# Diagonal score tiles split by query halves, softmax division and row statistics moved to VectorE, loads of the Wo stage reordered

## The reference

```
q, k, v = x@Wq.T+bq, x@Wk.T+bk, x@Wv.T+bv          # 16 heads
scores  = (q . k) * 64**-0.5 * exp(-alpha*|i-j|)
attn    = softmax(scores) ; out = (attn @ v) @ Wo.T + bo
x = layernorm(x + out)
xq, wq  = fp4_quant_dequant of blocks of 16 along the last dim (scale = max|x|/6)
h = silu(xq @ wgate_q.T) * (xq @ wup_q.T)           # width 2816
x = layernorm(x + quant(h) @ wdown_q.T)
```

## Time and profile before

| | us |
|---|---|
| median of 3 runs (lowest to highest) | 1411.84 (1408.74 to 1412.66) |
| the profiled execution, time | 1410.03 |
| its span on the slowest core (cores 1391.1 to 1408.5) | 1408.5 |
| PE busy | 1183.9 (84%) |
| DVE busy | 1060.4 (75%) |
| ACT busy | 707.0 (50%) |
| POOL busy | 300.7 (21%) |

### The profile page before, as it was taken

One profiled execution on the slowest core, in us unless ns is written; L12 is line 12 of the kernel. 1 busy time (PEld: TensorE's weight loads), 2 busy tenths in 40 slices (PEclk: granted clock), 3 DMA queues, 4 the chain that ended last, 5 costly groups with the idle time before them and its releaser, 6 DMA issues.

```text
span 1408.5 us, 18014 instructions; the slowest of 8 cores (1391.1 to 1408.5 us)
## 1 busy us (share of the span) xinstructions
PE 1183.9 (84%) x5283; PEld 441.4 (31%) x5344; DVE 1060.4 (75%) x1360; ACT 707.0 (50%) x803; POOL 300.7 (21%) x513
## 2 busy tenths in 40 slices
PE   3959888888888888887886493899999999999993
PEld 1312222222222222222221131344444444444441
DVE  2778888888989887887897421549988888888870
ACT  1038767677777776777797343652211221122212
POOL 2002223232222232222322132420000110011001
PEclk9979999999999998999999696999999999999997
DMA  9564334344444533543446919683333242333321
GB/s 150 114 140 128 112 93 119 97 107 101 122 118 105 121 104 96 129 108 92 126 108 159 245 55 308 210 272 91 111 84 84 73 121 84 79 84 92 92 61 55
DMA packets 179315, 167.27 MB, mean 119 GB/s; under 512 B 141842, under 2 KB 141842, under 8 KB 178324
## 3 DMA queue, kind: packets, MB, share of 16 engines
q1 hardware_dynamic: 164132, 127.97, 34.1%
q0 software_dynamic: 15088, 38.16, 11.5%
HBM read 111.30 MB, written 34.34 MB: 103 GB/s over the span
## 4 chain that ended last, share of the span: by engine, by line
PE 45%; DVE 18%; issue 15%; DMA 11%; ACT 5%; POOL 3%; SPq 1%; DVEq 1%; POOLq 0%; ACTq 0%
PE ps L953 12%; PE ps L545 8%; PE ps L412 7%; PE ps L1022 6%; PE ps L466 4%; PE ps L485 4%; ACT PT L530 3%; DVE SD L498 3%; PE ps L407 3%; DMA den_scr<-AV 2%; DVE fr L232 2%; DMA cD<-den_scr 2%; DVE hb L237 2%; POOL stat L813 2%; DMA hb<-x 1%
## 5 line engine op out<-in xcount | busy, mean ns | idle before, releaser
L530 ACT ACTIVATE PT<-ps,tab 128x1024 bf16<-128x1024 f32 x384 | 410.0, 1117 | 115.4 <-PE ps L466 114.2
L545 PE MATMUL ps<-PT,V 128*128 128x512 bf16 x992 | 296.4, 392 | 6.9 <-issue 2.7
L466 PE MATMUL ps<-Q,KT 64*128 64x512 bf16 x768 | 180.6, 391 | 31.4 <-ACT PT L530 26.7
L485 PE MATMUL ps<-Q,KT 64*128 64x512 bf16 x256 | 100.1, 391 | 106.4 <-DVE SD L498 97.1
L498 DVE TENSOR_TENSOR SD<-ps,tab 128x512 f32<-128x512 f32 x256 | 174.0, 680 | 20.3 <-PE ps L485 13.9
L953 PE MATMUL ps<-wgT,x1qT 128*128 128x512 bf16 (+1 forms) x768 | 167.8, 362 | 3.5 <-ACT sg L963 3.0
L953 PE MATMUL ps<-wuT,x1qT 128*128 128x512 bf16 (+1 forms) x768 | 167.8, 362 | 0.0
L412 PE MATMUL ps<-xTs,wqk 128*128 128x512 bf16 x495 | 145.5, 408 | 24.9 <-DMA xTs<-xT 17.1
L1022 PE MATMUL ps<-wdT,hqT 128*128 128x512 bf16 x704 | 156.3, 382 | 2.7 <-DMA hqT<-hq 2.7
L530 ACT ACTIVATE PT<-SD 128x1024 bf16<-128x1024 f32 x128 | 135.6, 1059 | 7.7 <-DVE SD L498 7.5
L805 ACT ACTIVATE junk<-ring 128x1024 bf16<-128x1024 f32 x22 | 23.2, 1054 | 214.3 <-DVE ring L1030 205.1
(11 more groups left out here) (84 smaller groups left out, 1365.4 us busy)
## 6 DMA issues: line engine op xcount, KB each, us to landing
ring<-x_scr SPq DMA_DIRECT2D x32, 512.0 KB, 5.3
wst<-wg SPq DMA_DIRECT2D x22, 512.0 KB, 3.8
wst<-wu SPq DMA_DIRECT2D x22, 512.0 KB, 3.7
wst<-wd SPq DMA_DIRECT2D x16, 704.0 KB, 4.1
recD<-rec_scr POOLq DMA_DIRECT2D x64, 128.0 KB, 3.6
out<-ring POOLq DMA_DIRECT2D x16, 512.0 KB, 6.3
wg_scr<-wtr SPq DMA_DIRECT2D x22, 256.0 KB, 2.0
wu_scr<-wtr SPq DMA_DIRECT2D x22, 256.0 KB, 2.0
```

The lines of the kernel that those rows point to most:

```text
L466: tok = op(TE, k0, lambda e, r0=r0, half=half: e.matmul(out=pt[:, half * 512:(half + 1) * 512], lhsT=KT[hp % 2][r0:r0 + 64, kt * 128:(kt + ...
L485: tok = op(TE, k0, lambda e: e.matmul(out=pt, lhsT=KT[hp % 2][r0:r0 + 64, kt * 128:(kt + 1) * 128], rhs=QR[u % 3][0][r0:r0 + 64, :], start ...
L530: f = op(AC, k0, lambda e: e.activation(out=PT[ri], in_=src, func=AF.Exp, scale=scl), [tok, pt_free[ri], t_tab])
L545: tok = op(TE, ka, lambda e, half=half: e.matmul(out=ps_ab[half], lhsT=VV[g][:, kt, hp % 4, 8 * half:8 * half + 128], rhs=PT[ri][:, half * ...
```

## The change

1. **Diagonal tiles.** The 512 queries are halved. For each half only two of the four key tiles lie on the diagonal; the other two are before or after all its queries. These go the factored way, with a third prescaled copy of the queries (table strM, which adds one DVE instruction per unit and head pair): a step "F" holds two key tiles of 256 queries and takes two exponentials of 128x512. The rest, step "D", still passes through SD: 4 DVE multiplies of 128x512 per unit instead of 8, 2 exponentials instead of 4. Matmuls of these steps have 256 columns, twice as many of them.
2. **Division** (L636 now) on DVE, at key ka+9.5, where ka is the key of the unit's last product with V (the last unit's at ka+23).
3. **Quantisers** are no longer spread evenly: `fill_gaps` replays the recorded DVE instructions with nominal durations (`durs`) and puts the chain's instructions where the nominal time leaves room.
4. **Wo stage.** The statistics come from `bn_stats` and `bn_aggr` on DVE (`layer_norm_w`), two small DVE instructions, two on POOL. The x row buffers wrow lie where the weight quantisers' buffers were, and the rows are loaded as soon as those are free. The loads of wuT follow after tiles 9, 11, 13, 14 and 15. The first product of stage G into hb waits for all stores of x1. `start_x1` of tiles 0 and 1 comes after tiles 7 and 10 (before: 4 and 6).
5. SBUF places and small tables follow from it.

```diff
-            tiles[u] = [k for i in range(4) for k in nd[3 * i:3 * i + 3] + [di[i]]]
+            nd = [("N", k) for k in range(NTT) if k not in di]
+            steps[u] = (nd[0:3] + [("F", di[0], di[1])] + nd[3:6] + [("D", di[0], di[1])]
+                        + nd[6:9] + [("F", di[2], di[3])] + nd[9:12] + [("D", di[2], di[3])])
+        BUF = [(j - (j > 7)) % 2 for j in range(16)]
...
+        durs = []
...
-                for n, ok, st in ((1, c > 0, strB), (2, c < 3, strA)):
+                for n, ok, st in ((3, True, strM), (1, c > 0, strB), (2, c < 3, strA)):
...
-                    rhs=Qs[r0:r0 + 64, :], start=True, stop=True,
-                    tile_position=(r0, 0)), need if half == 0 else [], signal=half == 1)
-            slot_last[hp] = tok
-            q_last[u] = tok
-            s_tok[(u, j)] = (tok, pt, None, k0, buf)
+            if need_d:
+                dt = bank(DB)
+                q0 = 256 * (b // 2)
+                h = j % 4
+                tok = d_a[0] = score(u, 4 * qc + b, h, 0, q0, q0 + 256,
+                                     dt[:, 256 * h:256 * h + 256], k0, need_d, True)
+            if st[0] == "N":
+                order = (1, 0) if j % 4 == 0 else (0, 1)
+                for half in order:
+                    tk = score(u, st[1], half, n, 0, 512, pt[:, half * 512:half * 512 + 512],
+                               k0, need if half == order[0] else [], half == order[1])
+            else:
+                q0 = 256 if j == 3 else 0
+                for i, k in enumerate(st[1:]):
+                    for half in range(2):
+                        c0 = 512 * half + 256 * i
+                        tk = score(u, k, half, n, q0, q0 + 256, pt[:, c0:c0 + 256], k0,
+                                   need if i + half == 0 else [], i + half == 2)
+            s_tok[(u, j)] = (tk, k0)
...
-            tok = op(TE, k0, lambda e: e.matmul(
-                out=pt, lhsT=KT[hp % 2][r0:r0 + 64, kt * 128:(kt + 1) * 128],
-                rhs=QR[u % 3][0][r0:r0 + 64, :], start=True, stop=True,
-                tile_position=(r0, 0)), need)
...
-            f = op(DV, km, lambda e: e.tensor_tensor(
-                out=SD[n][:, half * 512:(half + 1) * 512], in0=pt, in1=toep[:, x0:x0 + 512],
-                op=ALU.mult), [tok, t_tab, old, t_bo if u == 0 else None])
...
+            if j % 4 == 1:
+                n = b // 2
+                old = sd_exp[n]
+                km = max(k0 + 0.3, old.at + 0.02 if old is not None else -1e9)
+                x0 = 128 * (1 - b % 2)
+                f = dv(km, 0.69, lambda e: e.tensor_tensor(
+                    out=SD[n][:, 512 * (b % 2):512 * (b % 2) + 512].rearrange(
+                        "p (h q) -> p h q", h=2),
+                    in0=dt.rearrange("p (h q) -> p h q", h=2),
+                    in1=toep[:, x0:x0 + 256].unsqueeze(1).broadcast_to([128, 2, 256]),
+                    op=ALU.mult), [tok, t_tab, old, t_bo if u == 0 else None])
...
-                sd_exp[n] = f
-            else:
-                free_tok[buf], free_at[buf] = [f], k0
+                src = sc_ps[BUF[j]]
+                if st[0] == "N":
+                    m = 4 * qc - st[1] - 1 if st[1] < 4 * qc else st[1] - 4 * qc - 4
+                    scl = (sclB if st[1] < 4 * qc else sclA)[:, m:m + 1]
+                    f = op(AC, k0, lambda e: e.activation(
+                        out=PT[ri], in_=src, func=AF.Exp, scale=scl), need)
...
+                    for i in range(2):
+                        m = 1 - i if j == 3 else i
+                        scl = (sclB if j == 3 else sclA)[:, m:m + 1]
+                        part = lambda t, i=i: t.rearrange("p (h q) -> p h q", h=2)[
+                            :, :, 256 * i:256 * i + 256]
+                        f = op(AC, k0, lambda e, scl=scl, part=part: e.activation(
+                            out=part(PT[ri]), in_=part(src), func=AF.Exp, scale=scl),
+                            need if i == 0 else [], signal=i == 1)
+                free_tok[BUF[j]], free_at[BUF[j]] = [f], k0
...
                      + [t.at + 0.02 for t in need if t is not None])
...
+            if st[0] == "N":
+                prods = [(h, st[1], 512 * h, 0, 512) for h in range(2)]
+            else:
+                q0 = 256 if j in (3, 15) else 0
+                prods = [(h, k, 512 * h + 256 * i if st[0] == "F" else 256 * h + 512 * i, q0, 256)
+                         for i, k in enumerate(st[1:]) for h in range(2)]
+            for i, (h, k, c0, q0, w) in enumerate(prods):
+                tok = op(TE, ka, lambda e, h=h, k=k, c0=c0, q0=q0, w=w: e.matmul(
+                    out=ps_ab[h][:, q0:q0 + w], lhsT=VV[g][:, k, hp % 4, 8 * h:8 * h + 128],
+                    rhs=PT[ri][:, c0:c0 + w], start=first, stop=j > 12,
+                    skip_group_check=True), need if i == 0 else [], signal=i == len(prods) - 1)
             av_at[0] = ka
...
                     [t4, norm.get(u - 1)], sem=d_n4, k=16)
+            km = ka + 9.5 if u < NU - 1 else ka + 14.0 + 9.0
             for half in range(2):
                 lo = slice(64 * half, 64 * half + 64)
-                norm[u] = op(PO, ka + 5.8 + 0.1 * half, lambda e, half=half, lo=lo: e.tensor_tensor(
+                norm[u] = dv(km + 0.1 * half, 0.68, lambda e, half=half, lo=lo: e.tensor_tensor(
                     out=attnT[lo, hp, qc * QC:(qc + 1) * QC], in0=AVs[s][half][lo, :],
                     in1=recD[lo, :], op=ALU.mult), [t5])
...
-        spans = [(-30.0, at(0, 16))] + [(at(u, 1.9), at(u, 16.4)) for u in range(1, NU)]
-        spans[-1] = (spans[-1][0], at(NU - 1, 6))
-        room = sum(y - x for x, y in spans)
-
-        def place(f):
-
-            f *= room
-            for x, y in spans:
-                if f <= y - x:
-                    return x + f
...
+        U_US, P_US = 1.27, 0.95
+        t_of = lambda a: a * U_US if a > 0 else a * P_US
+        k_of = lambda t: t / U_US if t > 0 else t / P_US
+        durs.sort()
+        def fill_gaps(slack):
+            t, i, out, ka = t_of(-18.0), 0, [], -18.0
+            while i < len(durs) and durs[i][0] <= ka:
+                i += 1
+            for _, _, F in chunks:
+                for d, _ in quant_chain(wst[0][:, 0:F], wst[0][:, 0:F], wqo[0][:, 0:F], F, qr, qs):
+                    while i < len(durs) and t + d > t_of(durs[i][0]) + slack:
+                        t = max(t, t_of(durs[i][0])) + durs[i][1]
+                        ka = durs[i][0]
+                        i += 1
...
+                    nk = durs[i][0] if i < len(durs) else 1e9
+                    ka = max(ka + 1e-5, min(k_of(t), nk - 0.005))
+                    out.append((ka, k_of(t)))
+                    t += d
+            return out, k_of(t)
+        for slack in (0.2, 0.4, 0.6, 0.8, 1.0, 1.5, 2.0, 3.0, 5.0, 8.0):
+            places, q_end = fill_gaps(slack)
+            if q_end < at(NU - 1, 2):
+                break
+        places = iter(places)
+        nxt = next(places)
         w_read, w_tr, w_st = {}, {}, {}
...
+        ln_w = [0]
+        ln_done = [None] * 4
+        def layer_norm_w(x, tk):
+            o = 16 * (ln_w[0] % 4)
+            ln_w[0] += 1
+            c = lambda i, j=1: stat2[:, o + i:o + i + j]
+            for h in range(2):
+                tk, t = urgent(dve[0], 0.6, lambda e, h=h: e.bn_stats(
+                    out=c(6 * h, 6), in_=x[:, 512 * h:512 * h + 512]), [tk, ln_done[o // 16]])
+            tk, t = urgent(t, 0.1, lambda e: e.bn_aggr(out=c(12, 2), in_=c(0, 12)), [tk])
+            tk, t = urgent(t, 0.1, lambda e: e.tensor_scalar(
+                out=c(0), in0=c(12), scalar1=-1.0, scalar2=None, op0=ALU.mult), [tk])
+            tk, t = urgent(t, 0.1, lambda e: e.tensor_scalar(
+                out=c(1), in0=c(13), scalar1=EPS, scalar2=None, op0=ALU.add), [tk])
+            tk = fop(PO, t + 0.05, lambda e: e.tensor_tensor(
+                out=c(14), in0=c(1), in1=nhalf, op=ALU.pow), [tk])
+            tk = fop(PO, t + 0.06, lambda e: e.tensor_tensor(
+                out=c(15), in0=c(0), in1=c(14), op=ALU.mult), [tk])
+            t += 1.0
+            n = fop(AC, t + 0.05, lambda e: e.activation(
+                out=x, in_=x, func=AF.Identity, scale=c(14), bias=c(15)), [tk])
+            ln_done[o // 16] = n
+            return n, t + 1.3
         y_free = [(None, 0.0), (None, 0.0)]
         y_n = [0]
...
                 a = max(X0 - 8.0, pe[0] - 12.0,
                         w_free[s].at + 0.01 if w_free[s] else 0.0)
-                ld = fop(SP, a, lambda e: e.dma_start(out=row, in_=x_r[tt]),
-                         [w_free[s]] if w_free[s] else gate, sem=d_wl2[s], k=16)
+                ld = op(SP, a, lambda e: e.dma_start(out=row, in_=x_r[tt]),
+                        [w_free[s]] if w_free[s] else [prev] + t_ws, sem=d_wl2[s], k=16)
             y = y_n[0] % 2
...
             y_free[y] = (rt, t)
-            nt, t = layer_norm(row, t + 0.05, rt)
+            nt, t = layer_norm_w(row, rt)
```

(21 more changed lines are left out.)

199 lines of the change are left out of this document (89 added, 110 removed).

## The result

| | before | after |
|---|---|---|
| median of the runs (lowest to highest) | 1412.25 us | 1481.47 us (1476.12 to 1558.27) |
| ratio, 95% interval | | 1.0481 (1.0451 to 1.0511), slower |
| profiled execution, span | 1410.0, 1408.5 | 1476.12, 1474.5 |
| first copy of ps_ab | 111.61 | 110.12 |
| 29 periods, each | 648.9, 22.4 | 722.1, 24.9 |

A forecast was written before the change was run, and what follows sets the result against it. It took the kernel as bound by waits, the largest PE's 97.1 us for DVE's diagonal multiplies. Terms 7 + 0 + 1 - 29 + 13 = -8 gave 1402, against the median 1404 us; range 1377 to 1447.

The forecast's parts named there:

- R: Attention unit: time from DVE's copy of ps_ab to the division, through the wait for recD; taken as 14.7 us.
- PE's side: Attention: PE's wait for SD should be small, with a new one for the copy or projection banks there.
- Rival D: Attention, faster: only load counts, the wait is hidden, period about 20.3 us; sum -76, 1336 us; chance 0.05.
- the last leg: Attention, from recD's issue to the division: DVE now idle there, so 14.7 taken between 15.4 and 13.35.
- rival C: Attention, faster: the chain is quick, 13.8 us from copy to division; sum -34, 1378 us; chance 0.15.
- W: Attention unit: DVE's work from the division to the next copy; forecast 7.9 us each (7.3 to 8.9).
- +7: Attention, 29 periods: 29 x 14.7 + 230 = 656 us against 648.9.
- Rival A: Attention, slower: the quantiser's own transfers, tied to the unit, meet recD; R = 15.5, sum +16, 1428 us; chance 0.30.
- The burst: Attention, period at the burst of loads: reciprocal at +27, division about +38, 43.7 us against 44.0: 0.
- The last period: End of attention: R + 1.2 + 4.5 against 19.45 us: +1.
- The Wo stage: Between attention and G: 69 us, just over PE's 64, against 98.2: -29.
- The start of G: G(0) to G(1): second x1qT lands late behind wdT, at G+34 against G+21.2 before: +13.

The follow-up runs named there:

- e1: The changed kernel with the two divisions of a unit given back to POOL: 1370.91 us, ratio 0.9716.
- e3: The changed kernel with the division still on DVE but 17.5 keys behind the copy instead of 9.5, behind the next unit's copy: 1356.49 us, ratio 0.9619.
- e5: The changed kernel with the division on DVE 7.5 keys behind the copy instead of 9.5: 1538.53 us, ratio 1.0888.
- e5b: The changed kernel with the division on DVE 11.5 keys behind the copy instead of 9.5: 1413.92 us, ratio 0.9985.
- e11: e7 with the reciprocal and division of the last three units further back and the quantiser spread evenly: 1330.08 us, ratio 0.9443.
- e4: The changed kernel with the quantiser spread evenly by key instead of put into gaps, division still at 9.5 keys: 1483.08 us, ratio 1.0506.
- e9: The changed kernel without the weight loads of 56 of the quantiser's 60 chunks: 1427.21 us, ratio 1.0117.
- e2: The kernel before with only the two divisions of a unit moved from POOL to DVE, 9.5 keys behind the copy: 1517.11 us, ratio 1.0755.
- e6: e3 with the first two x1 quantisers three tiles earlier and the first gate products waiting only for x1 rows whose memory they take: 1349.55 us, ratio 0.9565.
- e7: e6 with the reciprocal 7.5 keys behind the copy instead of 5.5 and the division 18.5 instead of 17.5: 1342.90 us, ratio 0.9515.

## Why the prediction was wrong

**The mechanism was right.** "The period can't be shorter than R + 7.9", with DVE in strict order behind recD and PE behind DVE, is what e1, e3, e5 and e5b show. What it had wrong in kind is PE's side: its wait for the multiplies was to be small and grew from 55.5 to 96.7 us. Rival D (only load counts) was right to stand apart: with the wait gone the period is 21.2, or 20.65 in e11, against its 20.3. (Of the 97.1 us only 55.5 lie in the 29 periods, 1.9 each, which gives 20.5.) What sets the 21.2 was not tried.

**The step that failed is the size of R.** It was put at 14.7, "a value between these"; it was 16.44, 1.74 more in each of 29 periods, 50 us. As medians of the eight cores R was 16.1 before and 16.2 with the change: the lowering did not come at all. Two arguments had lowered it from the 15.9 that the trace gave as its mean.
- "In half of them the reciprocal came late in its own queue ... cD's landing sets it at 6.6 to 6.9." Measured 8.42. Before, cD landed 6.98 us after the copy on the mean of the 29 units, and the reciprocal stood 0.42 behind it: so only 0.4 of the 7.4 was DVE's queue. In the change cD itself landed at 8.04, a microsecond later, and the reciprocal 0.37 behind. DVE stood for cD in 21 of the 29 units, 42.6 us in all. With the quantiser spread evenly (e4) cD landed at 7.20 again, so this leg is where its tied transfers show; of R only 0.4 is gained by it.
- "In the last leg DVE will now stand idle too", with the quiet unit's 13.35 as the lower end. From recD's issue to the division it was 4.64 us before and 4.49 after: 0.15, not a whole microsecond. The last unit was as quick again (13.5), 2.9 under the mean; e9 puts 1.4 of that down to the loads, and the rest is open. The rule of the Trainium skill's page "SBUF — State Buffer" (SBUF: two separate sides), named for rival C, would have made this leg the quiet one. The change shows no such gain, nor does e4 (4.53); the 3.91 of e5 may hold some of it, and no run here separates that from the lower traffic.

**W was a little short.** 7.9 by the order and its prices, 8.46 measured, 16 us over 29 periods. DVE waits for no other engine there (its idle time between division and copy is 0.1 us a unit, all behind its own results), so it is the prices: the two divisions take 1.43 us from start to start, priced 1.2, and the two query copies 1.5 to 1.6, priced 1.33; the lines from 423.39 to 428.09 show both. In e4, e5 and e5b it is nearly the same (idle 0.14, 0.25 and 0.07); in e2, 1.7 of its 10.0 us are waits, nearly all for PE. The two errors, 50 and 16, are the whole distance of 66 us between the +7 forecast for the 29 periods and the +73.2 measured. Rival A had the right direction and, with R = 15.5, still too little; its cause, transfers tied to the unit, accounts for 0.4 us of R at most (e4).

**The burst**, 0: +2.0, with the division 38.5 us after the copy, 38 forecast (the reciprocal came at 24.3, not 27, so that the parts inside were less well placed than the sum). **The last period**, +1: +3.4.

**The Wo stage**, -29: -17.4. The terms held: BATCH_NORM_STATS2 took 0.69 us (0.65 taken), the tiles ran at PE's pace, the last one ended at 973.9, 73 us after the copy. Missing were a first tile of 6.41 us at the lower clock level, and 7.83 us for x1qT, whose transposition was issued at 968.58 among the wuT loads. With it earlier (e6, e7) PE goes from Wo to G without a stop, 71.0 and 69.9 us in the profiled cores: the forecast 69 within 2. The wait for x1qT is 7.0 and 7.8 us on two cores of the change and 1.8 to 3.6 on the other six.

**The start of G**, +13: +9.7, and the mechanism held. The second load of wdT landed at 1011.44 us, the second x1qT, behind it, at 1012.38, and G(1) began at 1012.62, 30.85 us after G(0) where 34 was forecast; as the median of the eight cores it is 33.9, and on all eight x1qT landed 0.8 to 1.6 us behind wdT. What the prediction named as its sign, PE standing over 8 us for x1qT, didn't show: the time was spent earlier, 7.07 us for the first product, which waited for the last x1 store, and 0.63 was left for x1qT (0 to 7.0 on the other cores). That wait lay inside, as the prediction said. It also held the second x1 quantiser on DVE, so that the transposition was issued only at 1002.00; but on every core it landed just behind wdT, so this by itself cost nothing that shows. The landings, of wdT (the second load, issued at 983.00, is the longest) and of x1qT (the second is the shortest):

```profile
DMA to landing us min/median/max: 26.3/27.4/28.4
...
DMA to landing us min/median/max: 10.4/11.7/12.9
```

**The range** went up to +35: R = 16.0, so +45 in the attention, with Wo at -20 and the burst 4 less. Measured are +73.2, -17.4 and +2.0. Of the attention's excess of 28, 13 are R = 16.44 and the rest is W; W had no room in the range at all, and the trace's own mean of R, 15.9, stood at its upper end.
